# One language-model layer with attention and a routed feed-forward, on one core: the router's running counts by three doubling additions on VectorE and two matrix products on TensorE, in place of nine products

## The reference

```python
logits = x2 @ Wr + br
probs = jax.nn.softmax(logits, axis=-1)
expert = jnp.argmax(probs, axis=-1)
oneh = jax.nn.one_hot(expert, e, dtype=x2.dtype)
pos = (jnp.cumsum(oneh, axis=0) * oneh).sum(-1).astype(jnp.int32) - 1
keep = pos < CAP
slot = expert.astype(jnp.int32) * CAP + jnp.minimum(pos, CAP - 1)
```

## Time and profile before

| | |
|---|---|
| median of 3 runs | 1514.93 us (1513.76 to 1516.85) |
| profiled execution | 1513.05 us, its span 1510.9 us |
| TensorE (PE) busy | 1472.9 us, 97% |
| TensorE weight loads (PEld) | 1361.5 us, 90% |
| ScalarE (ACT) busy | 1150.2 us, 76% |
| VectorE (DVE) busy | 1049.3 us, 69% |
| GpSimd (POOL) busy | 973.2 us, 64% |
| mean granted TensorE clock | 0.997 |

### The profile page before, as it was taken

One profiled execution on the slowest core, in us unless ns is written; L12 is line 12 of the kernel. 1 busy time (PEld: TensorE's weight loads), 2 busy tenths in 40 slices (PEclk: granted clock), 3 DMA queues, 4 the chain that ended last, 5 costly groups with the idle time before them and its releaser, 6 DMA issues. The chain is left out here.

```text
span 1510.9 us, 33846 instructions
## 1 busy us (share of the span) xinstructions
PE 1472.9 (97%) x11128; PEld 1361.5 (90%) x11128; DVE 1049.3 (69%) x2810; ACT 1150.2 (76%) x3471; POOL 973.2 (64%) x1051
## 2 busy tenths in 40 slices
PE   7789999999999999999999999998999999999999
PEld 3479999999999999999999999988999999999999
DVE  8987788787788887877887877774344333356665
ACT  7689888888888888888888888875555555555555
POOL 8575567887888788788878887675677655510000
PEclk9999999999999999999999999999999999999999
DMA  8223412111111211111111111012343234456665
GB/s 278 107 76 153 158 40 69 49 49 40 59 39 39 60 37 36 35 56 34 35 50 42 35 35 52 25 47 69 81 120 104 70 75 107 119 160 188 184 191 145
DMA packets 171503, 126.48 MB, mean 84 GB/s; under 512 B 30309, under 2 KB 154959, under 8 KB 171330
## 3 DMA queue, kind: packets, MB, share of 16 engines
q1 hardware_dynamic: 153794, 104.15, 22.9%
q0 software_dynamic: 17536, 20.17, 4.7%
HBM read 61.64 MB, written 78.66 MB: 93 GB/s over the span
## 5 line engine op out<-in xcount | busy, mean ns | idle before, releaser
L1190 ACT ACTIVATE expd<-masked,nmax 128x128 f32<-128x128 f32 x1024 | 395.8, 393 | 0.2 <-DVE nmax L1338 0.2
L958 POOL TENSOR_TENSOR prob<-expd,rtotal 128x1024 f32<-128x1024 f32 x128 | 243.1, 1899 | 127.4 <-DVE rtotal L1308 125.8
L1327 DVE COPY_PREDICATED masked<-off_diag,ps_s 128x1024 f32<-128x1024 int32 x128 | 175.1, 1368 | 143.6 <-PE ps_s L1088 143.6
L1128 PE MATMUL ps_o<-u,probT 128*128 128x128 f32 x2048 | 249.1, 275 | 0.0
L1128 PEld LDWEIGHTS ps_o<-u,probT 128*128 128x128 f32 x2048 | 239.1, 192 | 0.0
L1190 ACT ACTIVATION_READ_ACCUMULATOR expd<-masked,nmax 128x1 f32 x1024 | 196.6, 192 | 0.0
L1199 ACT ACTIVATE u<-ps_ut 128x1024 f32<-128x1024 f32 x128 | 131.4, 1026 | 64.7 <-PE ps_ut L1139 64.7
L1214 ACT ACTIVATE probT<-ps_ut 128x1024 f32<-128x1024 f32 x128 | 131.4, 1027 | 46.1 <-PE ps_ut L1096 39.8
L1275 DVE TENSOR_TENSOR w_lo<-ps_w,w_hi 128x512 fp32r<-128x512 f32 x256 | 164.3, 680 | 1.1 <-ACT w_hi L1223 1.1
L1223 ACT ACTIVATE w_hi<-ps_w 128x512 fp32r<-128x512 f32 x256 | 146.3, 596 | 15.8 <-PE ps_w L1114 9.6
L1338 DVE TENSOR_REDUCE nmax<-masked 128x8 f32<-128x1024 f32 x128 | 155.6, 1216 | 2.4
(11 more groups left out here) (258 smaller groups left out, 3871.2 us busy)
## 6 DMA issues: line engine op xcount, KB each, us to landing
turned<-x2T SPq DMA_DIRECT2D x32, 256.0 KB, 2.2
answers_sp<-zeros SPq DMA_DIRECT2D x16, 512.0 KB
answers_fq<-zeros SPq DMA_DIRECT2D x16, 512.0 KB
xT<-turned SPq DMA_DIRECT2D x56, 128.0 KB, 2.5
sh_back<-answers_sp SPq DMA_DIRECT2D x56, 128.0 KB, 2.3
sh_back<-answers_fq SPq DMA_DIRECT2D x56, 128.0 KB, 2.5
out<-res SPq DMA_DIRECT2D x56, 128.0 KB, 2.1
h_sb<-in_L_tok_weight SPq DMA_DIRECT2D x12, 512.0 KB, 6.4
```

The costliest lines, as they stand in the source:

```text
L958: nc.gpsimd.tensor_tensor(prob[k % 2][:, :].rearrange("p (g j) -> p g j", g=H), expd[k % 2][:, :].rearrange("p (g j) -> p g j", g=H), rtot ...
L1128: mm = nc.tensor.matmul(ps_o[:, 0:D], probT[k % 2][:, g * N:(g + 1) * N], u[k % 2][:, g * D:(g + 1) * D], start=(g == 0), stop=(g == H - 1))
L1190: ins = nc.scalar.activation(expd[(k - 1) % 2][:, g * N:(g + 1) * N], masked[(k - 1) % 2][:, g * N:(g + 1) * N], ACT.Exp, bias=nmax[(k - 1 ...
L1327: nc.vector.copy_predicated(masked[k % 2][:, :].rearrange("p (g j) -> p g j", g=H), off_diag[:, :].unsqueeze(1).to_broadcast([P, H, N]), p ...
```

## The change

Let c be the one-hot block of a tile. The sum of the blocks ahead of tile t within a batch is made on VectorE by doubling: `pairs[t] = c[t-1] + c[t-2]`, `fours[t] = pairs[t] + pairs[t-2]`, and then `pairs[t] = fours[t] + fours[t-4]`, each over all 9 blocks (144 columns, bf16). Zero blocks ahead of the data serve as the blocks before the batch. TensorE then makes two products of 144 columns: triangle times `chosen`, and ones times `pairs`. The reduction `key` moves from at 1 to the end of the step before. The SBUF for the new blocks comes from `zeros`: 8 rows in place of 10, so 20 fills in place of 16, of the same total size.

```diff
-ZERO_ROWS = 10
+ZERO_ROWS = 8
...
-        self.chosen = sb("chosen", [P, (BATCH + 1) * RE], BF16)
+        self.chosen = sb("chosen", [P, (2 + BATCH + 1) * RE], BF16)
+        self.pairs, self.fours = sb("pairs", [P, (2 + BATCH + 1) * RE], BF16), sb("fours", [P, (4 + BATCH + 1) * RE], BF16)
...
-                    for t, value in ((C.power, -0.5), (C.ones, 1.0), (C.tri, 1.0), (C.carry, 0.0), (C.chosen, 0.0), (C.var, 1.0)):
+                    for t, value in ((C.power, -0.5), (C.ones, 1.0), (C.tri, 1.0), (C.carry, 0.0), (C.chosen, 0.0), (C.pairs, 0.0), (C.fours, 0.0), (C.var, 1.0)):
...
-        chosen, carry, rank, mv1, mv2, var = C.chosen, C.carry, C.rank, C.mv1, C.mv2, C.var
+        BLOCKS = (BATCH + 1) * RE
+        before, pairs, fours, chosen = C.chosen, C.pairs, C.fours, C.chosen[:, 2 * RE:]
+        carry, rank, mv1, mv2, var = C.carry, C.rank, C.mv1, C.mv2, C.var
...
                     nc.tensor.matmul(ps_o[:, CUM_COL:end], C.tri[:, :], chosen[:, :], start=True, stop=False)
-                    for d in range(1, BATCH + 1):
-                        mm = nc.tensor.matmul(ps_o[:, CUM_COL + d * RE:end], C.ones[:, :], chosen[:, 0:(BATCH + 1 - d) * RE],
-                                              start=False, stop=(d == BATCH))
-                    mm.then_inc(S["cum"], 1)
+                    nc.tensor.matmul(ps_o[:, CUM_COL:end], C.ones[:, :], pairs[:, 2 * RE:], start=False, stop=True).then_inc(S["cum"], 1)
...
+                    yield
+                    link.wait()
+                    link.inc(nc.vector.tensor_reduce(key[:, :], by_expert(work2), X_AXIS, ALU.max))
                 if at == 1:
                     link.wait()
-                    link.inc(nc.vector.tensor_reduce(key[:, :], by_expert(work2), X_AXIS, ALU.max))
+                    link(nc.vector.tensor_tensor(by_expert(chosen)[:, 0:BATCH * BANKS, :], rank[:, :].unsqueeze(1).to_broadcast([P, BATCH * BANKS, E]),
+                                                 over_experts(key), ALU.is_equal))
+                    link.inc(nc.vector.tensor_tensor(pairs[:, 2 * RE:], before[:, RE:RE + BLOCKS], before[:, 0:BLOCKS], ALU.add))
                     yield
                     link.wait()
-                    nc.vector.tensor_tensor(by_expert(chosen)[:, 0:BATCH * BANKS, :], rank[:, :].unsqueeze(1).to_broadcast([P, BATCH * BANKS, E]),
-                                            over_experts(key), ALU.is_equal).then_inc(S["chosen"], 1)
+                    link(nc.vector.tensor_tensor(fours[:, 4 * RE:], pairs[:, 2 * RE:], pairs[:, 0:BLOCKS], ALU.add))
+                    nc.vector.tensor_tensor(pairs[:, 2 * RE:], fours[:, 4 * RE:], fours[:, 0:BLOCKS], ALU.add).then_inc(S["chosen"], 1)
```

## The result

The changed kernel takes 1518.17 us (median of 11 runs, 1516.18 to 1523.48) against 1514.52 us of the kernel before beside it (11 runs, 1512.00 to 1517.08): ratio 1.0026, 95% interval 1.0018 to 1.0034. It is slower by 4 us, where 1.9 us less was forecast, and it lies above the range of 1511.6 to 1517.5 us. The profiled execution has a span of 1516.5 us (before: 1510.9).

What follows compares the result with a forecast made beforehand. TensorE, busy 799.96 of 800 us in `attention`, was taken as the bound. Products -3.1, waits for `h1` +0.7 and the last batch +0.5 sum to -1.9 us: 1513.0 us from 1514.93, range 1511.6 to 1517.5.

Steps and rivals of the forecast that it cites:

- Two more memsets of some 150 columns in `setup` and a shorter one of `zeros` cancel out.: In the setup: the added memsets and the shorter one were costed together at nothing.
- A released product starts about 0.05 us behind the end of its releaser: TensorE in a batch: delay from the end of the releasing instruction to the product's start, 0.05 us.
- The margin: In the second batch: room between the end of `h1` and the counting products, after release, 0.40 us.
- The delay of `h1`, 0.45 us: VectorE between scores' copy and `h1`: added work makes `h1` 0.45 us later, giving TensorE 0.05 us wait a batch.
- one of 0.07: VectorE in a batch: the second addition is pushed 0.07 us later by GpSimd's addition L945.
- the products' gain: TensorE's counting products, two in place of nine: 0.22 us won a batch, 3.1 us for batches 1 to 14.
- the lower price of an addition: VectorE's bf16 additions cost by bytes: 0.15 us to the next start, 0.25 to a dependent one.
- rival 2: Additions cost by columns, `h1` 0.60 late, wait 0.20 to 0.25 us a batch: +0.6 us, 1515.5; chance 0.18.
- the last batch: At the last batch, without cover: three additions lengthen TensorE's wait by 0.75 us, products return 0.22, net cost 0.53 us.
- the fills at nothing: Twenty fills of 8 rows for sixteen of 10: same bytes, last one later but in time, costed at nothing.
- nothing lost in the fourteenth batch: In the fourteenth batch the margin is 0.70 us, so the later `h1` costs TensorE nothing.
- Rival 3: GpSimd's gather locks out the first addition, `h1` 1.1 late, wait 0.7 us in 13 batches: +6.5 us, 1521.4; chance 0.12.

Runs made afterwards that it cites:

- experiment 2: Changed kernel with the memsets of `pairs` and `fours` moved late in the setup, where GpSimd is idle; 1513.84 us, ratio 0.9989 to the kernel before.
- 4: Kernel before with only the setup side of the change (buffers, 8-row fills, two more memsets), those memsets placed late; 1513.11 us, ratio 0.9995.
- 5: Kernel before with its memset of `chosen` cut into twelve of 12 columns, same bytes, no new buffer; 1516.48 us, ratio 1.0011.
- 3: Kernel before with only the fills changed, 8 rows in place of 10, and a shorter `zeros`; 1514.93 us, ratio 0.9996.
- experiment 8: Changed kernel with the two memsets late and, in the last batch alone, nine products and no additions; 1514.65 us, ratio 0.9998.
- Experiments 1: Kernel before with only the setup side of the change: two early memsets, wider `chosen`, 8-row fills, nine products kept; 1517.12 us, ratio 1.0009.

## Why the prediction was wrong

- **The step that failed: "Two more memsets of some 150 columns in `setup` and a shorter one of `zeros` cancel out."** The prediction set durations against each other and did not ask where they stand. The two memsets take 0.4 us at 23.2 us; the shorter `zeros` gives back 0.22 us at 42.4, long behind. In the profiles they cost 3.3 us at the first scores, because GpSimd's product then starts 1.0 us ahead of VectorE's masked copy and not 1.4, and the copy is passed over twice. Experiments 2 and 4 take the memsets away from there, 5 makes the lock-out without them, and 3 clears the fills. No row of the setup stood in the prediction.
- **"A released product starts about 0.05 us behind the end of its releaser"** was read from a release by `chosen`, and carried over to `h1`. Behind `h1` it is 0.14 or 0.15 us in all of the 13 batches. The margin was 0.30, not 0.40. Why the two releases differ is open.
- **The delay of `h1`, 0.45 us**, measured 0.59 (0.85 in the fifth batch). The additions cost what was said; two collisions with GpSimd come in where one of 0.07 was counted. The one of `chosen` with `prob` stood in the prediction's own numbers: it lets `prob` end at 245.08 + 1.89 + 0.20 = 247.17 and `chosen` start at 245.85 + 1.25 = 247.10. Together this is a wait of 0.28 to 0.30 us a batch (0.46 in the fifth) in place of 0.05, thus +3.7 us from the first to the fourteenth batch in place of +0.7. The products won 2.9 to 3.1 us there, and the three executions show +0.5 to +0.9 us in place of the forecast -2.2.
- **Right:** the products' gain (0.22 to 0.24 us a batch); the lower price of an addition (0.23 us; rival 2, with a wait of 0.20 to 0.25, came nearest to the wait, for the wrong reason); the last batch (+0.81 of wait, forecast +0.75, less 0.22, and 0.6 us on the path by experiment 8); the fills at nothing; nothing lost in the fourteenth batch. Rival 3 fell: `pairs` lasts 0.24 us beside the gather. Its mechanism, GpSimd holding VectorE, was the one that decided, but in the setup.
- **Not foreseen:** the half clock at the drain, 1.6 us in two of three profiled executions. What decides whether it comes was not tried, and that the change brings it is not shown.

The mechanism of the setup is shown; its size in the timed runs is not settled. By the traces the changed kernel should lose 3.7 to 4.8 us before the first count, 0.4 to 0.9 in the batches and 0.2 or 1.8 behind them. The runs say 4. Experiments 1 and 5, with the setup's loss alone, say 1.4 and 1.7 us, each by 1.4 to 1.7 either way, below the 3.0 and 3.2 of their profiles (first counts at 195.52 and 195.68, before 192.49). But from the changed kernel to experiment 2, where only the memsets move, the ratio falls by 0.0037, which is 5.6 us. Experiment 2 should even be slower than the kernel before by its batches and last batch, and it is 1.7 us faster. The mean granted clock of its timed runs is 0.997, that of the changed kernel's two sets 0.995 and that of the kernel before 0.995 to 0.996, so a part of this may be the clock; no run parts the two. Timed runs have no trace, and the setup's course varies with the landing of the numbers. How often the kernel before has a slow setup for other reasons stays open.

## What to carry to other kernels

An instruction that is cheap by its duration is not free by its place: where VectorE and GpSimd both read SBUF in long instructions, read the timelines of both side by side around every instruction that you add, in the setup too, and put it where neither engine has such a neighbour. Before counting on a margin, measure the release behind that very kind of instruction, since here it was a tenth of a microsecond longer and a quarter of the margin of 0.40. When VectorE has idle time, put new work in it and ahead of whatever starts GpSimd: the same four instructions cost, with the products' gain taken off, +0.04 to +0.07 us a batch behind the scores' copy, -0.21 ahead of the reciprocal, and +1.1 between the two.

## What the runs showed of the hardware

- **Who gets in at a handover.** In eleven profiled executions VectorE's masked copy begins while GpSimd's `mixed` product runs and must wait for it. Where it began 1.40 to 1.43 us behind the product's start (six) it got in at the product's end and lasted 1.65 to 1.67 us; where it began 1.00 to 1.06 us behind (five) GpSimd's next two instructions, which followed without a gap, went first and it lasted 4.86 to 4.93 us. Nothing in between was seen, and why the earlier one loses is open. In the other three of the fourteen executions the copy began ahead of the product and lasted 1.84 us, and the product 2.91 or 2.92. The Trainium skill ("SBUF — State Buffer", Who interferes with whom) says that the order of issue decides who blocks, and (of VectorE's modes with two ports) that whoever issues first gets the shared ports for the whole instruction while the other blocks fully. The rows agree that the loser stands still until the other's end. In the five they do not agree that the order of issue decides, since GpSimd's clamp at 27.07 was served ahead of a copy that stood there from 26.20.
- **An addition of two bf16 blocks of 144 columns** in SBUF lasts 0.23 us, one of f32 columns from PSUM 0.306. This agrees with the rule of the Trainium skill's page "VectorE: DVE Perf Modes" (The perf-mode tier table), two bf16 elements a cycle and one of f32, which the prediction named beside its sum. The two differ in SBUF or PSUM as well, and no run parts this from the type.
- **A held VectorE instruction ends 0.10 to 0.16 us behind the GpSimd one if it is short** (`pairs` 250.54 behind `prob` 250.44), and by most of its own length behind it if it is long (the copy by 1.15 to 1.17 us; undisturbed it lasts 1.29).
